# Third layer of a four-layer graph network: signals once per column pair or chunk, and the sum's own wait placed ahead of the fill

## The chip, the cores and the metric

One core of one Trainium2 chip. The metric is the device time of one execution in microseconds (us), as a median of runs. A core has five engines with queues of their own: TensorE (PE, matmuls), VectorE (DVE), ScalarE (ACT), GpSimd (POOL, which here issues the indirect transfers) and SyncE (SP, which issues the plain ones). They meet only through semaphores: an instruction may add one to a semaphore when it ends (`then_inc`), and a queue may stand until a semaphore has reached a number (`wait_ge`).

## The reference

Four graph layers run one after the other over 6250 nodes and 106250 edges that are sorted by destination; each adds its input and normalises. The change lies in the third, an attention with six heads:

```python
gl = (x @ W_l).reshape(n, H, F_OUT)
gr = (x @ W_r).reshape(n, H, F_OUT)
s = jax.nn.leaky_relu(gl[src] + gr[dst], NEG_SLOPE)
e = jnp.einsum('ehf,hf->eh', s, att)
m = jax.ops.segment_max(e, dst, num_segments=n)
p = jnp.exp(e - m[dst])
denom = jax.ops.segment_sum(p, dst, num_segments=n)
alpha = p / (denom[dst] + 1e-16)
msg = alpha[:, :, None] * gl[src]
out = jax.ops.segment_sum(msg, dst, num_segments=n)
```

## The kernel before

The edges lie as 128 rows (partitions) of 832 columns, and each layer walks over them in 52 chunks of 16 columns. In the third layer a chunk c passes through these stations.

GpSimd (`layer2_g`, `g2_chunk`) gathers the 64 source features of each column with one indirect transfer per column into one of five buffers XS. It waits until the buffer's last use is over, by semaphores p2 (DVE) and ap (ACT). SyncE loads the destination features that stand at the first edge of each node (`x2_chunk`).

DVE fills the destination features of the other edges (`fill2`, L1191): column j is column j - 1 times a flag plus the loaded value, so each depends on the one before. Fills run four chunks ahead of the sums. Their semaphore is f2.

TensorE transposes four columns at a time (`pt_t`, L1205), multiplies them with the weights (`pm_t`, L1220, three times), and sums up the heads' logits (`pe_t`, L1236, then `pf_t`, L1251). ACT drains each of these banks (L1212, L1227, L1244, L1256); the last hands over the logits by semaphore ab.

DVE makes the softmax of a chunk in six steps (`soft2`, L1306 to L1320, semaphore q2), a running maximum forth and back over the columns among them. ACT takes two exponentials of it (`exp2_a`, L1329 and L1330, semaphore ax) and copies the maxima into the result (L1335, semaphore am).

The features are then scaled with each head's weight into a result S2 of 16 x 396 numbers a row, twice buffered: four heads by DVE in products of two columns (`px2`, L1354, semaphore p2), two heads by ACT, one copy per column and head (`px2_a`, L1371, semaphore ap). DVE makes running sums over the columns (`step2`, L1385; for a chunk's first column L1383 after the carry L1342), each dependent on the one before, semaphore t2. SyncE stores the 3168 KB of the chunk.

The order is written out by hand. DVE's (`layer2_v`) per column of chunk c is: fill of chunk c + 4, sum of chunk c, on even columns the product of the next pair, and in columns 8 to 13 one softmax step of chunk c + 1. From chunk 48 on there are no fills. ACT's (`layer2_a`) is eighteen places per chunk with the bank drains of chunk c + 3, and between them 33 instructions of `px2_a`, so that column j's two copies lie at about place 18 (2j + 3) / 33; ab is given at place 10. In the order before a fill waits for the fill before it, and a sum for its products, its own column's copies and the sum before it, in this order behind the fill:

```python
for j in range(CH):
    if c + 4 < NCH:
        fill2(e, c + 4, j)
    step2(e, c, j)
    if j % 2 == 0 and j + 2 < CH:
        px2(e, c, j // 2 + 1)
```

Of the kernel before, what the change touches and what calls it, by code (L numbers as in the profile page):

```python
# [7 lines left out]
D = 64  # L8
# [65 lines left out]
def bc(a, shape):  # L74
    return a.broadcast_to(shape)
# [6 lines left out]
def build(nc, x, src, dst, et16, et8, w0, beta, wl, wr, att, bias2, w3, coeff, hbias, loopw, out):  # L82
# [22 lines left out]
    with ExitStack() as ctx:  # L105
        names = ["tu", "m3", "e8", "ata", "att", "ao", "ab", "ae", "am", "ap", "ar", "at", "ax", "bad", "bb", "edges", "f1", "f2", "fin", "fina", "flag", "fr",
# [1051 lines left out]
        def q2_at(c):  # L1158
            return 6 * c - 2 if c else 0

        def p2_end(c):

            return 9 * c + 8

        def g2_chunk(e, c):
            if c >= NX:
                e.wait_ge(S["p2"], p2_end(c - NX))
                e.wait_ge(S["ap"], 33 * (c - NX + 1))
            for j in range(CH):
                gather(xsv(c)[:, j, 0:D], xt2, Si[:, c * CH + j:c * CH + j + 1], f"g_{2 * (c % NX) + j // 8}")  # L1170

        def x2_chunk(e, c):
            if c >= 3:
                e.wait_ge(S["f2"], 16 * (c - 3) + 15)
            load(e, XB2[:, c % 3, :], xdv[:, c * CH:(c + 1) * CH, :].rearrange("p j d -> p (j d)"), f"x_{c % 3}")

        def fill2(e, c, j):
            if c == 0 and j == 0:
                return
            cur, prv = xsv(c), xsv(c - 1)  # L1180
            XBv = XB2[:, c % 3, :].rearrange("p (j d) -> p j d", j=CH)
            if c == 0 and j == 1:
                e.wait_ge(S["xdi"], 32)
            if j == 0 or (c == 0 and j == 1):
                e.wait_ge(S[f"x_{c % 3}"], 16 * len(range(c % 3, NCH, 3)) + 16 * (c // 3 + 1))
                if c >= NX:
                    e.wait_ge(S["p2"], p2_end(c - NX))
                    e.wait_ge(S["ap"], 33 * (c - NX + 1))
            if c or j > 1:
                e.wait_ge(S["f2"], 16 * c + j - 1)  # L1190
            v.scalar_tensor_tensor(out=cur[:, j, D:P], in0=cur[:, j - 1, D:P] if j else prv[:, CH - 1, D:P],  # L1191
                                   scalar=gf[:, c * CH + j:c * CH + j + 1], in1=XBv[:, j, :],
                                   op0=ALU.mult, op1=ALU.add).then_inc(S["f2"], 1)

        def pt_t(e, u):
# [4 lines left out]
            if q == 0:  # L1200
                e.wait_ge(S["f2"], 16 * c + 15)
# [44 lines left out]
        def pf_t(e, c):  # L1246
            e.wait_ge(S["ae"], c + 1)
            if c:
                e.wait_ge(S["q2"], q2_at(c - 1) + (5 if c > 1 else 4))
            for i in range(4):  # L1250
                m = t.transpose(PS[7][:, i * P:(i + 1) * P], ETs[:, i * P:(i + 1) * P], ident[:])  # L1251
            m.then_inc(S["pf"], 1)
# [39 lines left out]
        def soft2(e, c, i):  # L1292
# [5 lines left out]
            n = q2_at(c) + (i - 1 if c == 0 and i else i)  # L1298
            if n:
                e.wait_ge(S["q2"], n)  # L1300
            if i == 0:
                e.wait_ge(S["ab"], c + 1)
                e.wait_ge(S["bb"], 1)
                if c:
                    e.wait_ge(S["am"], c)
# [16 lines left out]
            m.then_inc(S["q2"], 1)  # L1322

        def exp2_a(e, c):
            n_ = H * (CH + 1) if c else H * CH
            e.wait_ge(S["q2"], q2_at(c + 1))
            if c:
                e.wait_ge(S["p2"], p2_end(c - 1))
            s.activation(pw2[:, 0:n_], pf2[:, c % 2, 0:n_], ACT.Exp).then_inc(S["ax"], 1)  # L1329
# [5 lines left out]
            s.copy(s2v(c)[:, :, HW:].rearrange("p j h -> p h j"), mb2).then_inc(S["am"], 1)  # L1335

        def carry2(e, c):

            pq = pw2[:, H * CH:H * CH + H]
            e.wait_ge(S["ax"], 2 * c + 1)  # L1340
# [4 lines left out]
        def px2(e, c, k):  # L1345
# [4 lines left out]
            if k == 0:  # L1350
                e.wait_ge(S["ax"], 2 * c + 1)
                if c >= 2:
                    e.wait_ge(S[f"s_{c % 2}"], stored_before(2, c % 2) + 16 * (c // 2))
            v.tensor_tensor(s2v(c)[:, cols, 0:n * 65].rearrange("p j (h d) -> p j h d", h=n)[:, :, :, 0:D],  # L1354
                            bc(xsv(c)[:, cols, 0:D].unsqueeze(2), [P, 2, n, D]),
                            bc(pe_[:, cols, 0:n].unsqueeze(3), [P, 2, n, D]), ALU.mult).then_inc(S["p2"], 1)

        def px2_a(e, c, i):

            Sv, pe_ = s2v(c), p2v(c)  # L1360
            if i == 0:
                if c >= 2:
                    e.wait_ge(S[f"s_{c % 2}"], stored_before(2, c % 2) + 16 * (c // 2))
                    e.wait_ge(S["p2"], p2_end(c - 2) + 1)
                e.wait_ge(S["ax"], 2 * c + 2)
                s.copy(Sv[:, :, 0:HW].rearrange("p j (h d) -> p j h d", h=H)[:, :, :, D].rearrange("p j h -> p h j"),
                       pe_).then_inc(S["ap"], 1)
# [3 lines left out]
            s.activation(Sv[:, j, h * 65:h * 65 + D], xsv(c)[:, j, 0:D], ACT.Copy, scale=pe_[:, h, j:j + 1]).then_inc(S["ap"], 1)  # L1371

        def step2(e, c, j):
            if c == 0 and j == 0:
                return
            Sv = s2v(c)
            if j % 2 == 0 or (c == 0 and j == 1):
                e.wait_ge(S["p2"], p2_end(c) - 7 + j // 2)
            e.wait_ge(S["ap"], 33 * c + 1 + 2 * (j + 1))
            if c or j > 1:  # L1380
                e.wait_ge(S["t2"], 16 * c + j - 1)
# [8 lines left out]
        def layer2_v(e):  # L1390
# [7 lines left out]
            for c in range(NCH):  # L1398
# [3 lines left out]
                for j in range(CH):  # L1402
                    if c + 4 < NCH:
                        fill2(e, c + 4, j)
                    step2(e, c, j)
                    if j % 2 == 0 and j + 2 < CH:
                        px2(e, c, j // 2 + 1)
                    if c + 1 < NCH and j >= CH - 8 and j - (CH - 8) < 6:
                        soft2(e, c + 1, j - (CH - 8))
                    if c == NCH - 1 and j < 13:  # L1410
                        if j == 0:
                            e.wait_ge(S["am"], NCH)
# [43 lines left out]
        def layer2_y(e):  # L1456
# [4 lines left out]
            for c in range(NCH):  # L1461
                if c + 5 < NCH:
                    x2_chunk(e, c + 5)
                e.wait_ge(S["am"], c + 1)
# [858 lines left out]
```

## Time and profile before

| | |
|---|---|
| runs | 4820.8, 4825.5, 4825.6 us, median 4825.5 us |
| profiled execution, span from first to last instruction | 6172.5 us (a time around the span is not given) |
| busy in it | PE 1601.1, DVE 2873.7, ACT 1131.4, POOL 3511.2 us |
| third layer in it | about 3100 to 4750 us |
| DMA | 529.62 MB, mean 86 GB/s |

The profiled execution is 28% longer than the runs, so its durations of single instructions and its waits have to be told apart: the table's first line is what is to be forecast, and the rows below are from the second. A line of the timeline is a start, a length and an operation, with the idle time of the engine ahead of it in brackets. A length runs from start to the confirmed end; the next instruction of an engine may start before that. So the pace of an engine is read from start to start.

### The profile page before, as it was taken

Reading aid. Unit: us, or ns where it says so; the run is one execution under the profiler, and the core shown is the slowest. Engines: PE = TensorE matmul, PEld = TensorE weight load, DVE = VectorE, ACT = ScalarE, POOL = GpSimd, SP = SyncE. Lnnn points to the kernel's source line nnn. Section 1 sums busy time; section 2 is a strip of 40 time slices with the busy share of each in tenths; the row PEclk is TensorE's granted clock in tenths of the full one; section 3 lists DMA queues with packets and bytes.
Section 4 is the critical chain, followed back from the end, with each engine's and each line's share of the span. In section 5 each row is a group of like instructions: output and inputs, shape, how many; then the busy total and the mean of one; then the engine's idle time right before and its main releaser. Section 6 shows DMA issues by size and latency. Waiting matters only on the chain.

```text
span 6172.5 us, 31606 instructions
## 1 busy us (share of the span) xinstructions
PE 1601.1 (26%) x6543; PEld 810.8 (13%) x6543; DVE 2873.7 (47%) x7569; ACT 1131.4 (18%) x3424; POOL 3511.2 (57%) x3636
## 2 busy tenths in 40 slices
PE   5531110000000000003376566656564500000002
PEld 1421110000000000001122222222221400000001
DVE  2344444124345455444255555555556632443435
ACT  1100000000000000001155555555555500000000
POOL 4356666756666666664634544454452576666764
PEclk7765555555555555556688888888887655555555
DMA  4211222221222222221123333333334221222222
GB/s 139 106 53 62 67 64 71 67 81 54 58 64 71 62 69 68 64 71 37 49 106 118 140 138 123 130 139 134 118 140 154 69 67 55 64 79 63 79 63 78
DMA packets 185944, 529.62 MB, mean 86 GB/s; under 512 B 70454, under 2 KB 75170, under 8 KB 169480
## 3 DMA queue, kind: packets, MB, share of 16 engines
q1 hardware_dynamic: 65816, 395.51, 16.9%
q0 software_dynamic: 117696, 129.81, 9.2%
q10 hardware_dynamic: 2224, 2.13, 0.1%
q14 instruction: 151, 1.24, 0.1%
q8 instruction: 57, 0.93, 0.1%
HBM read 185.57 MB, written 341.44 MB: 85 GB/s over the span
## 4 chain that ended last, share of the span: by engine, by line
DVE 39%; another core or an unknown queue 27%; issue 14%; PE 11%; ACT 6%; POOL 3%; DMA 0%; DVEq 0%; ACTq 0%; POOLq 0%
DVE AR L1672 11%; DVE AR L514 5%; DVE ps L779 5%; PE ps L1220 4%; POOL AR L190 2%; ACT AR L1371 2%; PE ps L1236 2%; DVE AR L850 2%; DVE AR L1385 2%; ACT AR L1227 1%; DVE AR L364 1%; DVE AR L1662 1%; PE ps L680 1%; DVE AR L803 1%
## 5 line engine op out<-in xcount | busy, mean ns | idle before, releaser
L190 POOL DMA_INDIRECT AR<-xt,Si x2496 | 2404.4, 963 | 1715.2 <-issue 744.3
L190 POOL DMA_INDIRECT AR<-y,R x752 | 711.3, 946 | 531.1 <-issue 228.7
L1385 DVE SCALAR_TENSOR_TENSOR AR<-AR,gf 128x390 f32<-128x390 f32 x780 | 484.2, 621 | 665.8 <-ACT AR L1371 469.9
L1220 PE MATMUL ps<-AR,WLR 128*128 128x512 f32 x1248 | 690.3, 680 | 152.2 <-ACT AR L1227 113.0
L1672 DVE SCALAR_TENSOR_TENSOR AR<-AR,gf 128x128 f32<-128x128 f32 x831 | 295.0, 355 | 470.8 <-DVE AR L1672 386.9
L1371 ACT ACTIVATE AR<-AR 128x64 f32<-128x64 f32 x1664 | 495.4, 346 | 0.0
L1227 ACT ACTIVATE AR<-ps 128x512 f32<-128x512 f32 x624 | 368.5, 591 | 231.3 <-remote 168.1
L779 DVE SCALAR_TENSOR_TENSOR ps<-ps,gf,AR 128x64 f32<-128x64 f32 x831 | 241.9, 291 | 288.2 <-remote 168.4
L514 DVE SCALAR_TENSOR_TENSOR AR<-AR,gf 128x64 f32<-128x64 f32 x831 | 237.2, 285 | 263.6 <-DVE AR L514 173.3
L190 POOL DMA_INDIRECT AR<-s,endi x196 | 215.7, 1101 | 179.5 <-issue 113.4
L1220 PEld LDWEIGHTS ps<-AR,WLR 128*128 128x128 f32 x1248 | 242.2, 218 | 462.2 <-issue 342.1
L1354 DVE TENSOR_TENSOR AR<-AR,ps 128x512 f32<-128x512 f32 x416 | 282.8, 680 | 6.7 <-ACT ps L1329 6.7
L850 DVE SCALAR_TENSOR_TENSOR AR<-AR,gf 128x65 f32<-128x65 f32 x780 | 217.2, 278 | 95.9 <-remote 58.0
L1191 DVE SCALAR_TENSOR_TENSOR AR<-AR,gf 128x64 f32<-128x64 f32 x831 | 229.7, 276 | 48.5 <-DVE AR L1191 20.4
L828 ACT ACTIVATE ps<-AR 128x17 f32<-128x17 f32 (+1 forms) x52 | 9.8, 188 | 1262.0 <-remote 602.9
L364 DVE TENSOR_TENSOR AR<-AR,ps 128x1568 bf16<-128x1568 int32 x52 | 92.7, 1784 | 302.9 <-remote 279.9
L372 PE MATMUL ps<-AR 128*98 128x64 bf16 x832 | 80.1, 270 | 547.3 <-DVE AR L366 419.8
L1742 PE MATMUL ps<-ident,AR 128*128 128x128 f32 x1 | 0.5, 475 | 808.7 <-DVE AR L1672 808.7
L1991 ACT ACTIVATE AR<-AR 128x7 f32<-128x7 f32 x7 | 1.5, 208 | 1113.0 <-DVE AR L632 1050.4
L1236 PE MATMUL ps<-AR,A 128*32 128x512 f32 x1248 | 204.9, 604 | 0.0
L1016 PE MATMUL ps<-AR,ones 128*128 128x384 f32 (+1 forms) x6 | 3.7, 759 | 718.6 <-DVE AR L967 718.6
L883 PE MATMUL ps<-AR,ones 128*128 128x128 f32 x2 | 0.8, 502 | 698.3 <-DVE AR L868 698.3
(326 smaller groups left out, 3045.4 us busy)
## 6 DMA issues: line engine op xcount, KB each, us to landing
s<-AR SPq DMA_DIRECT2D x51, 3168.0 KB
AR<-xd SPq DMA_DIRECT2D x104, 512.0 KB
s<-AR SPq DMA_DIRECT2D x51, 1024.0 KB
AR<-xt,Si POOLq DMA_INDIRECT x2496
s<-AR SPq DMA_DIRECT2D x53, 512.0 KB
s<-AR SPq DMA_DIRECT2D x51, 528.0 KB
xd<-AR SPq DMA_DIRECT2D x52, 512.0 KB
y<-AR SPq DMA_DIRECT2D x24, 1024.0 KB
```

What stands on the lines that cost most here:

```text
L190: g.indirect_dma_start(out=o, out_offset=None, in_=table, in_offset=bass.IndirectOffsetOnAxis(ap=idx, axis=0)).then_inc(S[sem], 16)
L514: v.scalar_tensor_tensor(out=buf[:, j, :], in0=buf[:, j - 1, :] if j else prev[:, CH - 1, :], scalar=gf[:, c * CH + j:c * CH + j + 1], in1 ...
L779: v.scalar_tensor_tensor(out=xf1(c, j), in0=xf1(c, j - 1) if j else xf1(c - 1, CH - 1), scalar=gf[:, c * CH + j:c * CH + j + 1], in1=XBv[: ...
L850: v.scalar_tensor_tensor(out=Sv[:, j, 0:65], in0=Sv[:, j - 1, 0:65] if j else Sp[:, CH - 1, 0:65], scalar=gf[:, c * CH + j:c * CH + j + 1] ...
L1191: v.scalar_tensor_tensor(out=cur[:, j, D:P], in0=cur[:, j - 1, D:P] if j else prv[:, CH - 1, D:P], scalar=gf[:, c * CH + j:c * CH + j + 1] ...
L1220: t.matmul(PS[2 + k % 3][:], WLR[:, ch * P:(ch + 1) * P], XT2[:, u % 6, :], start=True, stop=True).then_inc(S["pm"], 1)
L1227: s.activation(RL2[:, u % 5, ch * 512:(ch + 1) * 512], PS[2 + k % 3][:], ACT.Relu).then_inc(S["ar"], 1)
L1236: m = t.matmul(PS[6][32 * q:32 * q + 32, :], w_, m_, start=(ch == 0), stop=(ch == 3))
L1354: v.tensor_tensor(s2v(c)[:, cols, 0:n * 65].rearrange("p j (h d) -> p j h d", h=n)[:, :, :, 0:D], bc(xsv(c)[:, cols, 0:D].unsqueeze(2), [P ...
L1371: s.activation(Sv[:, j, h * 65:h * 65 + D], xsv(c)[:, j, 0:D], ACT.Copy, scale=pe_[:, h, j:j + 1]).then_inc(S["ap"], 1)
L1385: m = v.scalar_tensor_tensor(out=Sv[:, j, 0:HW], in0=Sv[:, j - 1, 0:HW], scalar=gf[:, c * CH + j:c * CH + j + 1], in1=Sv[:, j, 0:HW], op0= ...
L1672: v.scalar_tensor_tensor(out=cur[:, j, :], in0=cur[:, j - 1, :] if j else prv[:, CH - 1, :], scalar=gf[:, c * CH + j:c * CH + j + 1], in1= ...
```

## The change

Inside the third layer signals are dropped and those left stand for more. A product signals only for the first and last pair of a chunk (three p2 steps a chunk with the carry, nine before). Of the scaled copies only the last of a pair of columns signals (8 a chunk, 33 before), and the sum of an even column waits for both columns' copies. Fills from the sixth chunk on signal once a chunk. Of the softmax only the last step signals, of the two exponentials the second, and semaphore am is gone. What is dropped is covered by the wait for the sum before: that wait now stands at the head of each column, ahead of the fill and the softmax step, and the softmax step has moved from behind the sum and product to ahead of the sum.

```diff
-        def q2_at(c):
-            return 6 * c - 2 if c else 0
+        def f2_at(c):
+
+            return 16 * c + 15 if c < 5 else 75 + c
 
         def p2_end(c):
 
-            return 9 * c + 8
+            return 3 * c + 2
 
         def g2_chunk(e, c):
             if c >= NX:
                 e.wait_ge(S["p2"], p2_end(c - NX))
-                e.wait_ge(S["ap"], 33 * (c - NX + 1))
+                e.wait_ge(S["ap"], 8 * (c - NX + 1))
...
             if c >= 3:
-                e.wait_ge(S["f2"], 16 * (c - 3) + 15)
+                e.wait_ge(S["f2"], f2_at(c - 3))
...
                     e.wait_ge(S["p2"], p2_end(c - NX))
-                    e.wait_ge(S["ap"], 33 * (c - NX + 1))
-            if c or j > 1:
+                    e.wait_ge(S["ap"], 8 * (c - NX + 1))
+            if c < 5 and (c or j > 1):
                 e.wait_ge(S["f2"], 16 * c + j - 1)
-            v.scalar_tensor_tensor(out=cur[:, j, D:P], in0=cur[:, j - 1, D:P] if j else prv[:, CH - 1, D:P],
-                                   scalar=gf[:, c * CH + j:c * CH + j + 1], in1=XBv[:, j, :],
-                                   op0=ALU.mult, op1=ALU.add).then_inc(S["f2"], 1)
+            m = v.scalar_tensor_tensor(out=cur[:, j, D:P], in0=cur[:, j - 1, D:P] if j else prv[:, CH - 1, D:P],
+                                       scalar=gf[:, c * CH + j:c * CH + j + 1], in1=XBv[:, j, :],
+                                       op0=ALU.mult, op1=ALU.add)
+            if c < 5 or j == CH - 1:
+                m.then_inc(S["f2"], 1)
...
-                e.wait_ge(S["f2"], 16 * c + 15)
+                e.wait_ge(S["f2"], f2_at(c))
...
-                e.wait_ge(S["q2"], q2_at(c - 1) + (5 if c > 1 else 4))
+                e.wait_ge(S["q2"], c)
...
-            n = q2_at(c) + (i - 1 if c == 0 and i else i)
-            if n:
-                e.wait_ge(S["q2"], n)
+            if c == 0:
+                vc.hold()
             if i == 0:
                 e.wait_ge(S["ab"], c + 1)
                 e.wait_ge(S["bb"], 1)
-                if c:
-                    e.wait_ge(S["am"], c)
                 m = v.tensor_copy(Bf[:, :, 1:CH], bc(Bn[:, c * CH + 1:(c + 1) * CH].unsqueeze(1), [P, H, CH - 1]))
...
                 m = v.scalar_tensor_tensor(out=pq, in0=Sp[:, CH - 1, HW:], scalar=Bn[:, c * CH:c * CH + 1],
                                            in1=mb2[:, :, 0], op0=ALU.add, op1=ALU.subtract)
-            m.then_inc(S["q2"], 1)
+            if i == (5 if c else 4):
+                m.then_inc(S["q2"], 1)
+            elif c == 0:
+                vc.up(m)
...
             n_ = H * (CH + 1) if c else H * CH
-            e.wait_ge(S["q2"], q2_at(c + 1))
+            e.wait_ge(S["q2"], c + 1)
             if c:
                 e.wait_ge(S["p2"], p2_end(c - 1))
-            s.activation(pw2[:, 0:n_], pf2[:, c % 2, 0:n_], ACT.Exp).then_inc(S["ax"], 1)
+            s.activation(pw2[:, 0:n_], pf2[:, c % 2, 0:n_], ACT.Exp)
             s.activation(pf2[:, c % 2, 0:n_], pf2[:, c % 2, 0:n_], ACT.Exp).then_inc(S["ax"], 1)
             if c >= 2:
                 e.wait_ge(S[f"s_{c % 2}"], stored_before(2, c % 2) + 16 * (c // 2))
             if c >= 2:
                 e.wait_ge(S["p2"], p2_end(c - 2) + 1)
-            s.copy(s2v(c)[:, :, HW:].rearrange("p j h -> p h j"), mb2).then_inc(S["am"], 1)
+            s.copy(s2v(c)[:, :, HW:].rearrange("p j h -> p h j"), mb2)
...
-            e.wait_ge(S["ax"], 2 * c + 1)
+            e.wait_ge(S["ax"], c + 1)
...
             if k == 0:
-                e.wait_ge(S["ax"], 2 * c + 1)
+                e.wait_ge(S["ax"], c + 1)
...
+            m = v.tensor_tensor(s2v(c)[:, cols, 0:n * 65].rearrange("p j (h d) -> p j h d", h=n)[:, :, :, 0:D],
+                                bc(xsv(c)[:, cols, 0:D].unsqueeze(2), [P, 2, n, D]),
+                                bc(pe_[:, cols, 0:n].unsqueeze(3), [P, 2, n, D]), ALU.mult)
+            if k in (0, CH // 2 - 1):
+                m.then_inc(S["p2"], 1)
...
+                e.wait_ge(S["ax"], c + 1)
+                s.copy(Sv[:, :, 0:HW].rearrange("p j (h d) -> p j h d", h=H)[:, :, :, D].rearrange("p j h -> p h j"), pe_)
...
+            m = s.activation(Sv[:, j, h * 65:h * 65 + D], xsv(c)[:, j, 0:D], ACT.Copy, scale=pe_[:, h, j:j + 1])
+            if j % 2 and h == H - 1:
+                m.then_inc(S["ap"], 1)
 
         def step2(e, c, j):
             if c == 0 and j == 0:
                 return
             Sv = s2v(c)
+            if j == 0 or (c == 0 and j == 1):
+                e.wait_ge(S["p2"], p2_end(c) - 1)
             if j % 2 == 0 or (c == 0 and j == 1):
-                e.wait_ge(S["p2"], p2_end(c) - 7 + j // 2)
-            e.wait_ge(S["ap"], 33 * c + 1 + 2 * (j + 1))
-            if c or j > 1:
-                e.wait_ge(S["t2"], 16 * c + j - 1)
+                e.wait_ge(S["ap"], 8 * c + j // 2 + 1)
...
                 for j in range(CH):
+                    if c or j > 1:
+                        e.wait_ge(S["t2"], 16 * c + j - 1)
                     if c + 4 < NCH:
                         fill2(e, c + 4, j)
+                    if c + 1 < NCH and j >= CH - 8 and j - (CH - 8) < 6:
+                        soft2(e, c + 1, j - (CH - 8))
                     step2(e, c, j)
                     if j % 2 == 0 and j + 2 < CH:
                         px2(e, c, j // 2 + 1)
-                    if c + 1 < NCH and j >= CH - 8 and j - (CH - 8) < 6:
-                        soft2(e, c + 1, j - (CH - 8))
                     if c == NCH - 1 and j < 13:
-                        if j == 0:
-                            e.wait_ge(S["am"], NCH)
                         mend_max_v(e, vc, 2, T2, H, B2, j)
...
             for c in range(NCH):
                 if c + 5 < NCH:
                     x2_chunk(e, c + 5)
-                e.wait_ge(S["am"], c + 1)
                 n = CH // 4 if c == NCH - 1 else CH
                 for j in range(0, CH, n):
                     e.wait_ge(S["t2"], 16 * c + j + n - 1)
```

## Rows read from the trace of the kernel before

**Rows 1.** the page: totals of the engines, and the busy tenths in 40 slices

```profile
PE 1601.1 (26%) x6543; PEld 810.8 (13%) x6543; DVE 2873.7 (47%) x7569; ACT 1131.4 (18%) x3424; POOL 3511.2 (57%) x3636
DVE  2344444124345455444255555555556632443435
POOL 4356666756666666664634544454452576666764
```

**Rows 2.** GpSimd's waits over the whole span: waiting instruction, releaser, total us, times, longest

```profile
POOL AR L190 <- issue: 1111.0, 3414, 55.9
POOL AR L190 <- ACT AR L1371: 607.3, 47, 52.3
POOL AR L190 <- DMA s<-AR: 171.3, 7, 92.7
POOL AR L190 <- DMA y<-AR: 84.2, 1, 84.2
POOL AR L190 <- DMA xt<-X: 49.0, 1, 49.0
```

**Rows 3.** timeline of GpSimd in the third layer: start, length, operation

```profile
3601.71 0.94 POOL L190 DMA_INDIRECT AR<-xt,Si  x1 [0.30 <-issue]
3602.96 0.94 POOL L190 DMA_INDIRECT AR<-xt,Si  x1 [0.31 <-issue]
```

**Rows 4.** waits of all engines, 3150 to 4650 us

```profile
DVE AR L1385 <- ACT AR L1371: 450.7, 122, 10.6
ACT AR L1244 <- remote: 365.8, 46, 11.0
```

**Rows 5.** timeline of DVE in a dense stretch of the third layer

```profile
3615.07 0.35 DVE L1311 TENSOR_TENSOR_SCAN AR<-AR 128x96 f32<-128x96 f32 x1
...
3618.52 0.22 DVE L1320 SCALAR_TENSOR_TENSOR AR<-AR,Bn 128x6 f32<-128x6 f32 x1
3618.66 0.27 DVE L1191 SCALAR_TENSOR_TENSOR AR<-AR,gf 128x64 f32<-128x64 f32 x1
3618.86 0.61 DVE L1385 SCALAR_TENSOR_TENSOR AR<-AR,gf 128x390 f32<-128x390 f32 x1
3619.39 0.28 DVE L1191 SCALAR_TENSOR_TENSOR AR<-AR,gf 128x64 f32<-128x64 f32 x1
3619.59 0.61 DVE L1385 SCALAR_TENSOR_TENSOR AR<-AR,gf 128x390 f32<-128x390 f32 x1
3620.31 0.57 DVE L1342 TENSOR_TENSOR ps<-AR,ps 128x390 f32<-128x390 f32 x1
3620.79 0.68 DVE L1354 TENSOR_TENSOR AR<-AR,ps 128x512 f32<-128x512 f32 x1
3621.38 0.28 DVE L1191 SCALAR_TENSOR_TENSOR AR<-AR,gf 128x64 f32<-128x64 f32 x1
3621.58 0.55 DVE L1383 TENSOR_TENSOR AR<-AR,ps 128x390 f32<-128x390 f32 x1
3622.05 0.68 DVE L1354 TENSOR_TENSOR AR<-AR,ps 128x512 f32<-128x512 f32 x1
```

**Rows 6.** timeline of DVE in the fourth layer

```profile
5411.81 6.17 DVE L1672 SCALAR_TENSOR_TENSOR AR<-AR,gf 128x128 f32<-128x128 f32 x16
...
5504.00 0.35 DVE L1672 SCALAR_TENSOR_TENSOR AR<-AR,gf 128x128 f32<-128x128 f32 x1 [1.00 <-DVE AR L1672]
```

**Rows 7.** timeline of ACT beside rows 5

```profile
3618.26 0.37 ACT L1371 ACTIVATE AR<-AR 128x64 f32<-128x64 f32 x1
3618.77 0.26 ACT L1329 ACTIVATE ps<-AR 128x102 f32<-128x102 f32 x1
3618.97 0.27 ACT L1330 ACTIVATE AR<-AR 128x102 f32<-128x102 f32 x1
...
3621.20 0.57 ACT L1227 ACTIVATE AR<-ps 128x512 f32<-128x512 f32 x1
...
3622.15 0.58 ACT L1227 ACTIVATE AR<-ps 128x512 f32<-128x512 f32 x1
```

More of the change, by code:

```diff
@@ L105, in build @@
     with ExitStack() as ctx:
-        names = ["tu", "m3", "e8", "ata", "att", "ao", "ab", "ae", "am", "ap", "ar", "at", "ax", "bad", "bb", "edges", "f1", "f2", "fin", "fina", "flag", "fr",
+        names = ["tu", "m3", "e8", "ata", "att", "ao", "ab", "ae", "ap", "ar", "at", "ax", "bad", "bb", "edges", "f1", "f2", "fin", "fina", "flag", "fr",
                  "i0", "init", "kn", "lp", "ma", "mp", "mv", "n0", "n1", "n3", "na", "oe", "of", "ofo", "or", "orl", "ot",
@@ L1350, in px2 @@
             if k == 0:
-                e.wait_ge(S["ax"], 2 * c + 1)
+                e.wait_ge(S["ax"], c + 1)
                 if c >= 2:
                     e.wait_ge(S[f"s_{c % 2}"], stored_before(2, c % 2) + 16 * (c // 2))
-            v.tensor_tensor(s2v(c)[:, cols, 0:n * 65].rearrange("p j (h d) -> p j h d", h=n)[:, :, :, 0:D],
-                            bc(xsv(c)[:, cols, 0:D].unsqueeze(2), [P, 2, n, D]),
-                            bc(pe_[:, cols, 0:n].unsqueeze(3), [P, 2, n, D]), ALU.mult).then_inc(S["p2"], 1)
+            m = v.tensor_tensor(s2v(c)[:, cols, 0:n * 65].rearrange("p j (h d) -> p j h d", h=n)[:, :, :, 0:D],
[3 more added lines that the diff above has]
+                m.then_inc(S["p2"], 1)
         def px2_a(e, c, i):
@@ L1364, in px2_a @@
                     e.wait_ge(S["p2"], p2_end(c - 2) + 1)
-                e.wait_ge(S["ax"], 2 * c + 2)
-                s.copy(Sv[:, :, 0:HW].rearrange("p j (h d) -> p j h d", h=H)[:, :, :, D].rearrange("p j h -> p h j"),
-                       pe_).then_inc(S["ap"], 1)
+                e.wait_ge(S["ax"], c + 1)
+                s.copy(Sv[:, :, 0:HW].rearrange("p j (h d) -> p j h d", h=H)[:, :, :, D].rearrange("p j h -> p h j"), pe_)
                 return
@@ L1370, in px2_a @@
             h += HV
-            s.activation(Sv[:, j, h * 65:h * 65 + D], xsv(c)[:, j, 0:D], ACT.Copy, scale=pe_[:, h, j:j + 1]).then_inc(S["ap"], 1)
+            m = s.activation(Sv[:, j, h * 65:h * 65 + D], xsv(c)[:, j, 0:D], ACT.Copy, scale=pe_[:, h, j:j + 1])
+            if j % 2 and h == H - 1:
+                m.then_inc(S["ap"], 1)
         def step2(e, c, j):
```

## The prediction

> **What bounds the kernel now.** I read the totals and the forty slices first [rows 1]. GpSimd, which issues the gathers, is busy longest, 57% of the span. VectorE (DVE) follows with 47%. In the slices of the third layer (about 3100 to 4750 us, the stretch where DVE shows 5 and POOL 4 to 5) neither is near full. So the third layer, as profiled, waits for something else than its own busy time.
>
> The waits of that stretch say for what [rows 4]. DVE stands 450.7 us for ScalarE's (ACT) scaled copies at L1371, and ACT stands 365.8 us, 46 times in 46 chunks, before the copy at L1244 for a releaser that the trace does not name. That copy waits for TensorE alone. A chunk so takes 1500 / 46 = 32.6 us.
>
> I don't take it that this stands in an execution without the profiler. The span is 6172.5 us, the median of the runs 4825.5 us, so 1347 us exist only under the profiler. Another row shows such a stretch by itself: in the fourth layer sixteen sums, each waiting for the one before, take 6.17 us, and a little later the same instruction begins 1.00 us after its forerunner ended [rows 6]. DVE itself slows there for no reason in the code. I take TensorE's late signals for the same thing and look for the bound in the dense stretches, between the stalls.
>
> There the pace per chunk of 16 columns is this.
> GpSimd: one gather every 1.25 us (3601.71 to 3602.96) [rows 3], so 16 x 1.25 = 20.0 us.
> DVE: from start to start, a fill to the sum behind it takes 0.20 us, a sum to the next fill 0.53, a product to what follows 0.59, the carry 0.48, the softmax steps 0.14 to 0.27 (six of them, 1.1 together), and the last sum to the carry 0.72 [rows 5]. With 16 fills, 14 sums at 0.53, one at 0.72, the first column's at 0.47, 8 products and the carry: 3.2 + 7.4 + 0.7 + 0.5 + 4.7 + 0.5 + 1.1 = 18.1 us.
> ACT: one drain of a bank and two scaled copies in 0.95 us (3621.20 to 3622.15) [rows 7], 16 times, 15.2 us, and by estimate 1.3 us for the six single instructions of a chunk (0.2 us each as from L1329 to L1330 [rows 7], more for L1244): 16.5 us.
>
> How much of GpSimd's 20 us is real? GpSimd has 3636 instructions, all but a few of them transfers [rows 1]. Waits that no layer's pace can hide are 171.3, 84.2 and 49.0 us for transfers, and the longest single ones of L1371 and of "issue", 52.3 and 55.9 us: 412.7 us together [rows 2]. If the gathers set the pace elsewhere, one takes (4825.5 - 412.7) / 3636 = 1.21 us, and a chunk 19.4 us. That lies 1.3 us above DVE's 18.1. So my reading is: GpSimd sets the pace of the third layer, with DVE close behind.
>
> **The change part by part.**
> *Signals dropped* (most products, most scaled copies, fills from the sixth chunk on, five of six softmax steps, am, one of two ax). In the dense rows each instruction begins 0.03 to 0.1 us before the end of the one ahead, signal or not waited for [rows 5]. A signal is sent at an instruction's end, beside the next one. I find nothing to win, and take 0.
>
> *Waits dropped on DVE* (f2, q2, and for most columns p2 and ap). In the dense rows they are met long before: fills follow at 0.53 us behind a 0.61 us sum, the softmax step at 3618.52 right behind its sum [rows 5]. Saving 0. Bounds: no loss, as a wait less can't delay; a gain of at most the reading error of these rows, 0.01 us an instruction, which over 46 instructions and 47 chunks is 22 us, and only if DVE set the pace.
>
> *The sum's own wait moved ahead of the fill.* This is the part with a price. Today column j's fill stands between sum j-1 and the wait for it, and overlaps the sum's end. Now the fill queues behind the wait. Behind an even column a product lies in between (0.59 us), which hides it. Behind an odd column nothing does: 7 places per chunk (columns 2, 4 to 14; before column 0 lie the carry and a product). What such a wait costs has two rows. The chain of the fourth layer has (6.17 - 0.35) / 15 = 0.39 us from start to start for 0.35 us of work [rows 6], so length plus 0.04; a sum of 0.61 to 0.62 would be followed at 0.65 instead of 0.53: 0.12 us. The last sum before the carry is followed at 0.72 [rows 5]: 0.19 us, but that one waits for two semaphores. I take 0.12, since the fill waits for one. 7 x 0.12 = 0.84 us per chunk, 18.1 becomes 18.9. There are 47 chunks with fills behind chunk 0, so 39 us on DVE, 62 us by the upper row, and none if the fill could not overlap the sum in the first place. The four last chunks have no fills; there the wait stood in this place already.
>
> The rows show an instruction that starts 0.08 us before the sum ahead of it ends [rows 5]. The Trainium skill, VectorE: DVE Perf Modes, section "The DRAIN you can't avoid", says that the next operation does not start until the pipe is empty, and that dropping semaphores gains nothing. By the first half the moved wait would cost 0 and not 0.84 us per chunk. The trace speaks against that half. With the second half it agrees.
>
> *Softmax steps ahead of the sum, not behind.* Their number and length stay. The last one now ends one sum (0.53 us) earlier. In exchange it no longer shields the fill behind odd columns, which is counted above.
>
> Its first step also waits for the logits (ab) and now has column 8's sum and product queued behind it, which were ahead of it. ACT hands over ab at place 10 of its order and column 8's copies only after it, so the sum would stand there anyway: 0.
>
> *Pairs of scaled copies.* An even column now waits for both columns' copies, two more copies and perhaps a drain, up to 0.95 us [rows 7]. Both sums then run at once. While DVE is behind ACT nothing is lost. At a chunk's start the second pair of copies ends at about 3622.2, and the first column's sum begins at 3621.58 [rows 5, 7]; the softmax's end 0.53 us earlier makes up for it. Left is a delay of up to 1 us, once, ahead of the last pair of sums.
>
> *ax once*: the carry now waits for the second exponential, ended at about 3619.3, and starts at 3620.31 anyway. 0. *SP's wait for am dropped*: the store waits for the chunk's last sum, later anyhow. 0. *x2 loads and TensorE's f2 waits* name the same last fill. 0. *TensorE's wait for q2* ahead of L1251 names the step one column later; ACT's drain L1244, which it waits for too, stands in ACT's queue behind the exponential of that very softmax. 0. *p2 and ap for releasing a gather buffer* name the same last product and copy. 0.
>
> **Sum.** GpSimd's 19.4 us per chunk stay, DVE goes from 18.1 to 18.9 below it, the tail gets about 1 us. In the profiled execution it is no more: DVE stands 450.7 us idle for ACT in the stretch [rows 4], and 0.84 x 46 = 39 us go into that. Span 6172.5 plus 1; time 4825.5 plus 1.5, **4827 us**. A difference under 0.2% (9.7 us) is about what measurements of this kernel can't tell from none.
>
> **Rivals.**
> *A, slower: DVE sets the pace of the third layer.* Place: seven fills per chunk behind the moved wait. For it: DVE is within 1.3 us of GpSimd, by a division that assumes that gathers pace all other layers; where other layers have idle time too, a gather takes less than 1.21 us, and at 18.1 / 16 = 1.13 us DVE is even. From 18.9 / 16 = 1.18 us on it begins to cost. Against it: the profiled rate is 1.25. Price 47 x 0.84 = 39 us: 4865 us; between 1.13 and 1.18 a part of it.
> *B, faster: ACT's wait for the softmax lies on the path.* Its copy starts at 3618.26, the next could start 0.24 us later, and the exponential starts at 3618.77, right behind the last softmax step: 0.27 us of idleness [rows 7]. The step comes 0.53 us earlier now, so that goes. Should ACT's order of work set the pace (through TensorE's banks), 51 x 0.27 = 14 us are won: 4812 us. Against it: ACT's 16.5 us are the least of the three.
> *C: the trace's stall is real.* If TensorE's late signals stand outside the profiler too, all three engines have some 12 us per chunk to spare, and the time stays at 4825 us. It is a part of "same".
>
> **How the numbers follow.** My forecast with C 0.50, A 0.32, B 0.18. The range goes from B's 4810 to A's 4866. Faster by over 0.2%: 0.18; within: 0.50; slower: 0.32.
>
> **What would show it.** In the profile after, DVE's dense stretch should have a fill 0.65 us behind an odd column's sum instead of 0.53, 0.20 from fill to sum unchanged, and 0.6 behind a product. The gathers keep their 1.25 us. The exponential L1329 should no longer stand behind the softmax's last step. If the time falls by more than 14 us, signals or met waits have a price that these rows do not show. If it rises by more than 39, the wait for pairs has one. If fills follow odd sums at 0.53 still, my term is void.

## The result, and the profile after

Before: 4823.16 us (median of 4 runs, 4819.81 to 4825.64). After: 4790.42 us (4 runs, 4789.92 to 4791.97). The ratio is 0.9939, 95% interval 0.9927 to 0.9950: 33 us faster, where 4827 and a range from 4810 up were forecast. The changed kernel taken once more (e7) gave 4784.51 against 4814.37 us, ratio 0.9939 [0.9922, 0.9955].

One thing first, without which the numbers can't be read: within a set of runs taken together on one chip, the kernel before takes either 4808 to 4826 us or some 6030 to 6190 us, in each run of the set, and the profiled execution before the prediction looks like one of the second kind. I say quick and slow chips for short, though it isn't shown to be a property of the chip: e16 (slow) and e17 (quick), 12 minutes apart, both ran on what is numbered chip 9, which may or may not be the same one. A new profile of the kernel before, on a quick chip (e8), is what the changed kernel is set against here. (The two come from different sets, in which before took 4813.6 and 4823.2 us.) Totals of the engines, GpSimd's busy tenths in 40 slices and the gathers' group, kernel before on a quick chip:

```profile
span 4811.9 us, 31606 instructions
PE 1460.2 (30%) x6543; PEld 739.3 (15%) x6543; DVE 2848.1 (59%) x7569; ACT 1131.6 (24%) x3424; POOL 3536.0 (73%) x3636
POOL 6777777777777777776777777777744777777776
L190 POOL DMA_INDIRECT AR<-xt,Si x2496 | 2416.8, 968 | 809.3 <-issue 757.9
```

The same of the changed kernel:

```profile
span 4788.2 us, 30757 instructions
PE 1454.7 (30%) x6543; PEld 751.3 (16%) x6543; DVE 2862.1 (60%) x7569; ACT 1123.5 (23%) x3424; POOL 3508.8 (73%) x3636
POOL 6777777777777777776777777777654777777776
L190 POOL DMA_INDIRECT AR<-xt,Si x2496 | 2386.1, 956 | 811.5 <-issue 755.2
```

849 instructions are gone (31606 to 30757), yet DVE is not less busy. What fell is GpSimd's busy time, by 27 us, with the same 3636 instructions. From the first running sum of the third layer to the last go 1084.8 us before (2448.7 to 3533.5) and 1053.8 after (2451.9 to 3505.7): 31 us less. The gain lies there. The wait of [rows 2] for L1371, 607.3 us, is gone on a quick chip: from 2500 to 3400 us, inside the third layer, GpSimd stands for other engines 2 us before and 6 us after. Its groups of instructions in that stretch (count | busy us, mean ns | idle time before), first before (e8), then after:

```profile
L190 POOL DMA_INDIRECT AR<-xt,Si x686 | 692.7, 1010 | 209.1 <-issue 206.9 <-ACT AR L1371 2.1
```

```profile
L190 POOL DMA_INDIRECT AR<-xt,Si x710 | 683.9, 963 | 216.8 <-issue 210.9 <-DVE ps L1345 5.7 <-ACT AR L1375 0.3
```

Between two gathers lie the same 0.30 us in both. In 900 us after has 24 gathers more, for one reason: a gather takes 963 ns on average and not 1010. With 48 chunks of 16 gathers, 768 x 0.047 = 36 us. Summed gather by gather from 2450 to 3480 us, what they take beyond 945 ns is 50.4 us before and 15.8 after. GpSimd does set the pace, as forecast, but its pace depends on something that the change moves.

Answering to [rows 3] and [rows 5], the timeline of GpSimd and DVE in the kernel before on a quick chip (start, length; the wait of an engine in brackets):

```profile
2924.31 0.63 DVE L1385 SCALAR_TENSOR_TENSOR AR<-AR,gf 128x390 f32<-128x390 f32 x1 [0.78 <-ACT AR L1371]
2925.20 0.94 POOL L190 DMA_INDIRECT AR<-xt,Si  x1 [0.30 <-issue]
...
2927.50 0.62 DVE L1385 SCALAR_TENSOR_TENSOR AR<-AR,gf 128x390 f32<-128x390 f32 x1 [2.23 <-issue]
2927.70 1.25 POOL L190 DMA_INDIRECT AR<-xt,Si  x1 [0.30 <-issue]
...
2929.09 0.62 DVE L1385 SCALAR_TENSOR_TENSOR AR<-AR,gf 128x390 f32<-128x390 f32 x1
2929.25 1.47 POOL L190 DMA_INDIRECT AR<-xt,Si  x1 [0.30 <-issue]
...
2929.62 0.35 DVE L1314 TENSOR_TENSOR_SCAN AR<-AR 128x96 f32<-128x96 f32 x1
...
2938.54 0.62 DVE L1385 SCALAR_TENSOR_TENSOR AR<-AR,gf 128x390 f32<-128x390 f32 x1
2938.95 1.02 POOL L190 DMA_INDIRECT AR<-xt,Si  x1 [0.30 <-issue]
```

A gather with no sum under its start takes 0.94 us. One that starts 0.20 us after a sum takes 1.25 (0.31 more), one 0.41 us after 1.02. The one 0.16 us after a sum takes 1.47, but there a softmax step with two inputs in SBUF, the running maximum back over the columns (L1314), follows directly on the sum. And the changed kernel:

```profile
2906.12 0.68 DVE L1357 TENSOR_TENSOR AR<-AR,ps 128x512 f32<-128x512 f32 x1
2906.50 0.95 POOL L190 DMA_INDIRECT AR<-xt,Si  x1 [0.31 <-issue]
2906.91 0.62 DVE L1390 SCALAR_TENSOR_TENSOR AR<-AR,gf 128x390 f32<-128x390 f32 x1
2907.57 0.28 DVE L1192 SCALAR_TENSOR_TENSOR AR<-AR,gf 128x64 f32<-128x64 f32 x1
2907.75 0.95 POOL L190 DMA_INDIRECT AR<-xt,Si  x1 [0.30 <-issue]
2907.77 0.62 DVE L1390 SCALAR_TENSOR_TENSOR AR<-AR,gf 128x390 f32<-128x390 f32 x1
...
2919.84 0.22 DVE L1320 SCALAR_TENSOR_TENSOR AR<-AR,Bn 128x6 f32<-128x6 f32 x1
2919.98 0.62 DVE L1390 SCALAR_TENSOR_TENSOR AR<-AR,gf 128x390 f32<-128x390 f32 x1
2920.10 0.26 ACT L1332 ACTIVATE ps<-AR 128x102 f32<-128x102 f32 x1 [0.91 <-DVE AR L1320]
```

A sum that starts 0.02 us after the gather costs it nothing, nor does a product (one input in SBUF, one in PSUM) that starts 0.38 us ahead of one. The fill follows its sum at 0.66 us, as forecast. Sorted by where the sum starts against the gather over 2500 to 3400 us, the mean length of a gather in the kernel before is 1028 ns for a sum 0.45 to 0.40 us ahead, 1101 for 0.35 to 0.30, 1231 for 0.25 to 0.20, 1422 for 0.20 to 0.15, and 944 to 945 for sums 0.10 us ahead to 0.05 us behind.

One rule fits nearly all of them: the gather ends 0.94 us after a point that lies 0.48 to 0.50 us behind the sum's start (161 of the 187 gathers with a sum 0.10 to 0.45 us ahead). So the less the lead, the longer the gather. Where L1314 follows on the sum, that point lies 0.69 to 0.70 us behind its start (22 of 23 cases); 16 of the 21 gathers in the place with 1422 ns are such. The changed kernel has none of these, for its softmax step stands ahead of the sum.

In the changed kernel (e7, another profile of it) the cheap half of the costly places is as full as before (85 sums 0.45 to 0.40 or 0.35 to 0.30 us ahead, 93 before), but the dear half is nearly empty: 4 sums 0.25 to 0.10 us ahead, where before had 80.

That was a correlation in two traces. The Trainium skill, "SBUF — State Buffer", section "Who interferes with whom", says that a DVE instruction with two SBUF inputs contends with a GpSimd instruction that reads SBUF, and that issue order decides who blocks. The sum has two such inputs. A gather reads its indices (Si) there. These traces show one side only: a sum holds up a gather, but sums that start while a gather runs last 0.62 us like all others, and a sum less than 0.10 us ahead of a gather doesn't hold it.

### The profile page after: what moved, and what is told of

It reads as the page before. It is cut to its first block and busy times, and to the rows that moved or that the text cites. A ratio compares the mean times of both kernels' runs of the same rounds, so it can differ in the third digit from the quotient of the medians.

```text
span 4788.2 us, 30757 instructions
## 1 busy us (share of the span) xinstructions
PE 1454.7 (30%) x6543; PEld 751.3 (16%) x6543; DVE 2862.1 (60%) x7569; ACT 1123.5 (23%) x3424; POOL 3508.8 (73%) x3636
## 5 line engine op out<-in xcount | busy, mean ns | idle before, releaser
L190 POOL DMA_INDIRECT AR<-y,R x752 | 723.6, 962 | 238.1 <-issue 218.1
L1223 PE MATMUL ps<-AR,WLR 128*128 128x512 f32 x1248 | 609.4, 612 | 72.8 <-ACT AR L1230 72.8
L1666 DVE TENSOR_TENSOR AR<-AR,ps 128x2048 f32<-128x2048 f32 (+1 forms) x53 | 119.1, 2248 | 545.0 <-DMA AR<-xt,Si 545.0
L800 DVE TENSOR_TENSOR AR<-AR,ps 128x512 f32<-128x512 f32 x104 | 66.9, 684 | 437.2 <-DMA AR<-xt,Si 437.2
L1357 DVE TENSOR_TENSOR AR<-AR,ps 128x512 f32<-128x512 f32 x416 | 283.0, 680 | 6.8 <-ACT AR L1333 6.8
L190 POOL DMA_INDIRECT AR<-s,endi x196 | 215.9, 1101 | 76.7 <-issue 65.8
L1223 PEld LDWEIGHTS ps<-AR,WLR 128*128 128x128 f32 x1248 | 214.4, 192 | 324.1 <-issue 237.5
```

The source lines that it names most:

```text
L190: g.indirect_dma_start(out=o, out_offset=None, in_=table, in_offset=bass.IndirectOffsetOnAxis(ap=idx, axis=0)).then_inc(S[sem], 16)
L1223: t.matmul(PS[2 + k % 3][:], WLR[:, ch * P:(ch + 1) * P], XT2[:, u % 6, :], start=True, stop=True).then_inc(S["pm"], 1)
L1357: m = v.tensor_tensor(s2v(c)[:, cols, 0:n * 65].rearrange("p j (h d) -> p j h d", h=n)[:, :, :, 0:D], bc(xsv(c)[:, cols, 0:D].unsqueeze(2) ...
```

## The experiments

Two theories in the end, in the expectations from e12 on. S: sums with two SBUF inputs that start just ahead of a gather hold it up; the change moved them. G: signals and waits cost time themselves. The expectations of e1 to e11 were written before this was seen and use other letters: W says that ACT's wait for the softmax is a link of the loop that sets the pace, and S there is what is called G later.

**First round, slow chip** (before 6054.66 us, 15 runs; e1 itself 6062.85).

> The kernel before, unchanged, for a second profile that is hopefully not stretched. Theory W (ACT's wait for the softmax ahead of the exponential is a link of the loop DVE - ACT - TensorE): a chunk of the third layer takes 20.9 us (20.24 us of after plus 33 us / 48), GpSimd has to wait for the release of a buffer in most chunks, and ACT stands longer before L1329 than the 0.9 us of after, some 1.5 us. Theory S (the signals themselves cost time on ACT or DVE): ACT's copies or DVE's sums stand further apart from start to start than in after (0.24 and 0.53 us there).

The softmax step alone moved ahead of the sum and product:

```diff
                     if c + 4 < NCH:
                         fill2(e, c + 4, j)
+                    if c + 1 < NCH and j >= CH - 8 and j - (CH - 8) < 6:
+                        soft2(e, c + 1, j - (CH - 8))
                     step2(e, c, j)
...
-                    if c + 1 < NCH and j >= CH - 8 and j - (CH - 8) < 6:
-                        soft2(e, c + 1, j - (CH - 8))
```

> The kernel before with one thing of the change alone: the softmax step stands ahead of the sum and product of its column instead of behind them, all signals and waits kept. Theory W: nearly the whole gain, -25 to -35 us (4790 to 4798). Theory S: nothing, within 5 us of before.

Only the scaled copies signal once per pair of columns:

```diff
-            s.activation(Sv[:, j, h * 65:h * 65 + D], ...).then_inc(S["ap"], 1)
+            m = s.activation(Sv[:, j, h * 65:h * 65 + D], ...)
+            if j % 2 and h == H - 1:
+                m.then_inc(S["ap"], 1)
...
-            e.wait_ge(S["ap"], 33 * c + 1 + 2 * (j + 1))
+            if j % 2 == 0 or (c == 0 and j == 1):
+                e.wait_ge(S["ap"], 8 * c + j // 2 + 1)
```

> The kernel before with ACT's scaled copies signalling once per pair of columns (8 a chunk instead of 33) and the sum of an even column waiting for the pair, nothing else. Theory W: no gain, 0 to +10 us, as an even column starts later. Theory S: -10 to -33 us.

Only the wait for the sum before moved ahead of the fill:

```diff
                 for j in range(CH):
+                    if c or j > 1:
+                        e.wait_ge(S["t2"], 16 * c + j - 1)
                     if c + 4 < NCH:
                         fill2(e, c + 4, j)
...
-            if c or j > 1:
-                e.wait_ge(S["t2"], 16 * c + j - 1)
```

> The kernel before with the wait for the sum before moved ahead of the fill, nothing else. By the price of my prediction (0.12 us in 7 places of 47 chunks): +39 us if DVE is in the loop that sets the pace, which theory W says, so +20 to +45 us. Theory S with DVE off the path: 0.

Measured: softmax ahead 1.0084 [1.0056, 1.0112], pairs 0.9983 [0.9973, 0.9994], wait ahead 1.0075 [1.0050, 1.0100]. A single part made the kernel slower here, though the whole makes it faster on a quick chip. Why a slow chip's times don't answer the question shows in e1's waits, 3100 to 4200 us:

```profile
POOL AR L190 <- ACT AR L1371: 357.4, 35, 11.3
DVE AR L1385 <- ACT AR L1371: 276.8, 105, 8.9
ACT AR L1244 <- remote: 219.7, 33, 10.0
```

DVE stands for ACT's copies, ACT for something unnamed ahead of the copy of TensorE's logits (L1244), and GpSimd for 357 us of 1100; the gathers don't set the pace. Another slow chip (before 6177.64 us, 11 runs):

> The kernel before, unchanged, a look. On a chip that runs it in about 4823 us, theory W: 20.9 us per chunk of the third layer (after: 20.24), GpSimd waiting for buffers in most chunks, ACT standing about 1.5 us ahead of L1329 (after: 0.9). Theory S: ACT's copies or DVE's sums further apart than 0.24 and 0.53 us. On a chip that takes about 6050 us again: stalls as in the profile before, and no answer.

> The softmax step ahead of the sum, all signals and waits kept, once more. On a chip with before at about 4823 us, theory W: -25 to -35 us. Theory S: within 5 us. On a chip with before at about 6050 us: +0.8% again, as in e2.

e5 took 6188.08 us, e6 1.0041 [1.0026, 1.0057].

**Quick chips.** The changed kernel again:

> The changed kernel itself. On a chip with before at 4823 us: 4790 us again. On a chip with before at 6050 to 6180 us, where e2 to e6 were run: soft_early and wait_ahead gave +0.4 to +0.8% there and pairs -0.2%. If the change is the sum of its parts, after is 0 to +1.4% there; theory W, in which GpSimd's 20.2 us limit what can be gained on a quick chip and the stalls of the late signals rule on a slow one, says slower or the same; theory S (fewer signals are less work wherever signals are slow) says clearly faster there, by 1% or more.

4784.51 us, 0.9939 [0.9922, 0.9955]. It repeats the gain, with a span of 4779.8 us. Then, in one set of runs (before 4813.60 us, 22 runs), the kernel before in profile, the softmax step ahead, the pairs, and the changed kernel with its softmax step put back behind the sum (for which it keeps its own six q2 signals):

> The kernel before, unchanged, a look, hoped for on a chip that runs it in about 4820 us. Theory W: 20.9 us per chunk of the third layer (after: 20.24), GpSimd waiting for buffers in most chunks, ACT standing about 1.5 us ahead of L1329 (after: 0.9). Theory S: ACT's copies or DVE's sums further apart than 0.24 and 0.53 us.

> Before with the softmax step ahead of the sum, nothing else. With before at about 4820 us, theory W: -25 to -35 us. Theory S: within 5 us.

> Before with ACT's copies signalling once per pair, nothing else. With before at about 4820 us, theory W: 0 to +10 us. Theory S: -10 to -33 us.

```diff
...
+                    step2(e, c, j)
+                    if j % 2 == 0 and j + 2 < CH:
+                        px2(e, c, j // 2 + 1)
                     if c + 1 < NCH and j >= CH - 8 and j - (CH - 8) < 6:
                         soft2(e, c + 1, j - (CH - 8))
-                    step2(e, c, j)
-                    if j % 2 == 0 and j + 2 < CH:
-                        px2(e, c, j // 2 + 1)
```

> After with the softmax step put back behind the sum and product, where it stood before, and its own signals and waits with it; all else as in after. With before at about 4820 us, theory W: the gain is gone, 4815 to 4860 us (the wait ahead of the fill costs without its counterpart). Theory S: 4785 to 4792 us, the gain stays.

e8 took 4813.78 us, e9 4808.48, e10 4821.88, e11 4801.19. Each kernel's mean gather, 2500 to 3400 us, gives its span to some 7 us (e7 and e17 are from other sets of runs, in which before took 4814.37 and 4815.41 us). The estimate is 768 gathers times the difference to e8's 1010 ns:

| kernel | mean gather, ns | estimate, us | span to e8's 4811.9, us | third layer, us | ratio of times |
|---|---|---|---|---|---|
| e10 pairs | 1011 | +1 | +2.6 | 1091.8 | 1.0018 [1.0008, 1.0028] |
| e8 before | 1010 | 0 | 0 | 1084.8 | 1 |
| e9 softmax ahead | 994 | -12 | -9.7 | 1074.7 | 0.9992 [0.9982, 1.0002] |
| e11 after, softmax behind | 982 | -22 | -14.6 | 1071.4 | 0.9976 [0.9965, 0.9987] |
| e17 (below) | 968 | -32 | -26.4 | 1056.5 | 0.9947 [0.9930, 0.9963] |
| e7 changed kernel | 962 | -37 | -32.1 | 1052.5 | 0.9939 [0.9922, 0.9955] |

The pairs alone drop 25 of 33 signals a chunk and win nothing; the runs are 8 us longer, the span 3. The softmax step's place alone took 10 us off the span in the profiled execution, but only 5 off the median, which isn't clear of noise (0.9982 to 1.0002). With the rest of the change around it, it is worth 17 us (e11 to e7).

Theory W falls: it expected 25 to 35 us from e9 and no gain left in e11, and in e8 GpSimd stands 2 us of 900 for buffers, not in most chunks. The S of these expectations falls with e10, of which it expected 10 to 33 us. e11, at 4801.19 us, lies between what the two expected.

**Taking the cause away.** Everything of the kernel before stays, signals and waits too, but in columns 1 to 12 one input of the sum comes from PSUM. (The sum then leaves the scaled copies out in those columns.)

```diff
-                                           ..., in1=Sv[:, j, 0:HW],
+                in1 = bc(pw2[:, 0:1], [P, HW]) if j <= CH - 4 else Sv[:, j, 0:HW]
+                                           ..., in1=in1,
```

> The kernel before with one input of the sum in the third layer changed: in columns 1 to 12 of a chunk it adds one column of the exponentials, which lie in PSUM, in place of the scaled copies, so that only one of its inputs lies in SBUF (this leaves the sum over the scaled copies out of those columns; they are still written and still waited for). Same operation, same 390 elements, same waits and signals. Theory S (a sum that starts 0.1 to 0.5 us ahead of a gather holds it up until the sum has read its two SBUF inputs): gathers are held up in 4 of 16 columns at most, their mean length falls from 1.010 to about 0.96 us, and the kernel takes about 4780 us, 30 to 35 less than before, with every signal of before in its place. Theory G (the signals and waits themselves cost the time, and the gathers are long for a reason of their own): the mean stays at 1.00 to 1.01 us and the time within 0.2% of before.

> The same edit of the sum on the changed kernel (columns 1 to 12 leave the scaled copies out). Theory S: its gathers had only 0.30 us a chunk of delay left, so little is to be had: mean length 0.963 to about 0.95 us, time 4775 to 4785 us, and less than 10 us between this kernel and the same edit on the kernel before, where the two without the edit differ by 29. Theory G: the two still differ by about 29 us.

> The kernel before with one thing moved: the sum's wait for the sum before it stands ahead of the fill, every signal kept, as the change has it. Theory S: the fill starts 0.12 us later after each sum, which shifts the sums against the gathers but does nothing else; gathers' mean length between 0.98 and 1.01 us, time 4800 to 4820. If the wait's place alone made the changed kernel faster: 4790.

> The kernel before with both of the change's moves (the wait ahead of the fill, the softmax step ahead of the sum) and with every signal of before kept. Theory S has it that signals matter only through the places at which the sums start: with the order of the changed kernel but the waits of before, the mean length of a gather comes out between 0.963 and 0.994 us and the time between 4790 and 4808, and the two follow one line with the other kernels (some 42 us for each us of delay in a chunk). If signals cost time of their own: over 4808 at a delay of the gathers like the changed kernel's.

This was a slow chip once more (before 6058.28 us, 18 runs). Ratios: e12 1.0232 [1.0183, 1.0282], e13 1.0109 [1.0073, 1.0145], e14 1.0073 [1.0051, 1.0095], e15 1.0024 [1.0007, 1.0040]; all the times expected were for quick chips and are void. The lengths of the gathers still answer. Their means, 3100 to 4200 us, are 991 ns in e1 and 990 in e3 (pairs), but 974 in e4 and e14 (wait ahead), 972 in e2 (softmax ahead) and 982 in e15 (both): with every signal kept, either move alone changes how far the gathers are held up. GpSimd's group, 3100 to 4200 us, e1 and then e12:

```profile
L190 POOL DMA_INDIRECT AR<-xt,Si x574 | 568.6, 991 | 525.8 <-ACT AR L1371 357.4 <-issue 168.4
```

```profile
L190 POOL DMA_INDIRECT AR<-xt,Si x522 | 495.5, 949 | 646.8 <-ACT AR L1371 493.7 <-issue 153.1
```

991 falls to 949 ns. All that gathers take beyond 945 ns fell from 26.9 to 3.1 us. A sum 0.25 to 0.15 us ahead stretched a gather to 1205 and 1274 ns in e1, and to 944 in e12. So the hold-up comes from the second SBUF input. What it is worth needed a quick chip:

> The kernel of e12 again (the kernel before with one SBUF input of the sum in columns 1 to 12 replaced by a column in PSUM, which leaves the scaled copies out of the sum there), to have its time where the gathers set the pace. On the other chip the edit took the delay of the gathers from 26.9 to 3.1 us in 1100 us of the third layer. Theory S: mean length of a gather 0.945 to 0.96 us against 1.010, third layer 1040 to 1055 us against 1085, time about 4780 us against 4814, with every signal of before. Theory G: within 0.2% of before.

Slow again (before 6055.83; 1.0226 [1.0195, 1.0258]).

> The kernel of e12 and e16 once more (the kernel before with one SBUF input of the sum in columns 1 to 12 replaced by a column in PSUM, which leaves the scaled copies out of the sum there), for a chip on which the gathers set the pace. Theory S there: mean length of a gather 0.945 to 0.96 us against 1.010, third layer 1040 to 1055 us against 1085, time about 4780 us against 4814. Theory G: within 0.2% of before. On a chip like that of e16 (before about 6055 us), both expect what e16 gave, 1.02 times before, with gathers of 0.949 us.

A quick chip: 4788.35 us against 4815.41 (7 runs), ratio 0.9947 [0.9930, 0.9963], 27 us faster. Theory G, which expected the time within 0.2% of before, falls. Groups of GpSimd and of the sum, and the timeline of e17:

```profile
L190 POOL DMA_INDIRECT AR<-xt,Si x708 | 685.3, 968 | 215.8 <-issue 210.9 <-ACT AR L1371 4.3 <-DVE AR L1354 0.6
L1386 DVE SCALAR_TENSOR_TENSOR AR<-AR,gf,ps 128x390 f32<-128x390 f32 x531 | 328.8, 619 | 78.5 <-ACT AR L1371 54.0 <-issue 24.2
```

```profile
2907.75 0.62 DVE L1386 SCALAR_TENSOR_TENSOR AR<-AR,gf,ps 128x390 f32<-128x390 f32 x1 [0.41 <-ACT AR L1371]
2907.88 0.94 POOL L190 DMA_INDIRECT AR<-xt,Si  x1 [0.30 <-issue]
...
2917.54 0.61 DVE L1386 SCALAR_TENSOR_TENSOR AR<-AR,gf 128x390 f32<-128x390 f32 x1
2917.87 1.09 POOL L190 DMA_INDIRECT AR<-xt,Si  x1 [0.30 <-issue]
```

The sum is as long as before (619 ns, before 622), and yet one that starts 0.13 us ahead of a gather leaves it at 0.94 us. In column 15, where both inputs still lie in SBUF, a lead of 0.33 us gives 1.09. The same holds for the whole 900 us of this one trace: of the gathers that start 0.10 to 0.45 us after a sum, the 157 behind a sum with an input in PSUM take 0.94 to 0.96 us, and the 43 behind a sum with both in SBUF 1.03 to 1.39, 1.20 on average. That shows the cause. The time falls a little short of the 4780 us expected: the mean stayed at 968 ns, not under 960. Two thirds of what is left comes from these 43 in columns 13 to 15.

> The kernel of e13 again (the changed kernel with one SBUF input of the sum in columns 1 to 12 replaced by a column in PSUM, which leaves the scaled copies out of the sum there). On the quick kind of chip, where the kernel before takes about 4815 us, the same edit made that kernel 27 us faster, though every signal of it stood. Theory S: the changed kernel had little delay of gathers left, so it gains under 10 us by the edit (4780 to 4790 us), and the two edited kernels lie within 8 us of each other, where the unedited ones lie 29 to 33 us apart. Theory G: the two edited kernels are still 29 us apart (about 4760 us). On the other kind of chip (before about 6055 us) both expect what e13 gave, 1.011 times before.

This too met a slow chip (before 6059.32; 1.0077 [1.0051, 1.0103], mean gather 955 ns). So whether the two kernels come out equal once the cause is taken from both wasn't seen on a quick chip.

## Why the prediction was wrong, point by point

**GpSimd sets the pace: right.** It has 0.30 us between gathers and no wait to speak of in both kernels.

**A chunk of 19.4 us in the kernel before: the step that failed.** I divided the time by the number of transfers and got one rate, 1.21 us, for the whole kernel and for both versions. Undisturbed, a gather comes each 1.25 us, as [rows 3] said. In the third layer of the kernel before it came each (692.7 + 209.1) / 686 = 1.31 us, which is 21.0 us a chunk, and after each (683.9 + 216.8) / 710 = 1.27 us, 20.3 a chunk. So the term "GpSimd's 19.4 us per chunk stay" was wrong twice: it was 21.0 and not 19.4, and it didn't stay but fell by 0.7 us. Over 48 chunks that is 34 us, and that is the miss; my sum had no term by which the change could reach GpSimd's pace. The trace of before had it: the gathers' group from 3150 to 4650 us has a mean of 988 ns where [rows 3] show 0.94, and its timeline shows one of the long ones just behind the stretch of [rows 5]. The group first, then the timeline, both of the kernel before as profiled for the prediction:

```profile
L190 POOL DMA_INDIRECT AR<-xt,Si x738 | 729.0, 988 | 771.6 <-ACT AR L1371 555.0 <-issue 216.5
```

```profile
3625.68 0.63 DVE L1385 SCALAR_TENSOR_TENSOR AR<-AR,gf 128x390 f32<-128x390 f32 x1
...
3625.83 1.29 POOL L190 DMA_INDIRECT AR<-xt,Si  x1 [0.31 <-issue]
```

I took the clean rows for the pace and didn't ask what made the others longer.

**"1347 us exist only under the profiler": wrong.** On quick chips the profiled executions span 4779.8 to 4814.5 us, and on a slow one the kernel before takes 6033 to 6072 us in all 18 runs of a set. The stalls of [rows 4] and [rows 6] are a slow chip's: in the fourth layer's chain of [rows 6] 417 of 778 sums come 1.4 us after the one ahead, in e1 420, and in e8 none (0.5 at most). To read the pace from the dense stretches was sound; the reason given for it was not.

**The moved wait costs 0.12 us behind an odd column: right in size, and half the story.** From sum to fill the median start-to-start went from 0.535 to 0.654 us. It is the one term that I had as a loss, and rival A made 39 us of it. DVE did not set the pace: it still waits 45.8 us in 900 for the scaled copies (before 65.0). And a delay of DVE is not only a cost here, since it moves the sums against the gathers. I had also taken the Trainium skill, VectorE: DVE Perf Modes, section "The DRAIN you can't avoid", to be contradicted by the rows. The same section goes on to say that a next operation that isn't held starts earlier, and the 0.535 us behind a sum of 0.62 us agree with that.

**Dropped signals and waits are worth 0: upheld, not proven.** ACT's copies follow each other at 0.24 us with and without them, and e10 gained nothing from 25 signals less; the other dropped signals were never tried by themselves. e17, with all signals, has its third layer within 3 to 4 us of the changed kernel's (1056.5 to 1052.5 and 1053.8), and these fit the 6 ns between the mean gathers.

**Rival B, faster by ACT's wait: wrong mechanism.** It had the sign by luck: it said that the wait before the exponential goes, and it grew: in 900 us from 1.6 us to

```profile
ACT ps L1332 <- DVE AR L1320: 39.6, 44, 1.0
```

44 times 0.9 us, and the kernel is faster all the same. **Rival C** named stalls that quick chips don't have.

**What stays open.** Why this order makes the sums land in harmless places. Nearly all of the changed kernel's chunks repeat at 20.2 or 20.3 us, those of before wander between 19.5 and 23.7. That the softmax step's place enters is seen in e9 and e11; the moved wait by itself was seen to change the gathers on slow chips only (e4, e14), and so was the order of the changed kernel with all signals kept (e15). I had no way to foretell the places. Nor is it known what makes a chip slow, or why there most kernels with shorter gathers took longer.

## What to carry to other kernels

When the engine that sets the pace shows unequal lengths for equal instructions, sort them by what another engine does at their start before taking any of them for its rate. An edit that costs the other engine time can still win, if it moves that engine's instructions with two SBUF inputs away from the stretch just ahead of the pacing ones. And look at the clean and the mean length side by side: here 0.94 against 0.99 us was the whole case.

## What the runs showed of the hardware

- A sum of 390 elements with two inputs in SBUF that starts 0.10 to 0.45 us ahead of a gather on GpSimd holds it up until 0.48 to 0.50 us behind the sum's start in 161 of 187 cases of e8, so by 0.05 to some 0.4 us, and a sum less than 0.10 us ahead does not. With one input in PSUM the same sum does nothing to it (e12, e17). The rule of the Trainium skill on two SBUF inputs, cited above, agrees, and here issuing an indirect gather behaves as a GpSimd instruction that reads SBUF.
- Instructions with two SBUF inputs in close succession add up. With L1314 directly behind the sum the hold ends 0.69 to 0.70 us behind the sum's start. The two longest gathers of e8, 1.59 us, start between a fill 0.11 us ahead of them and a sum 0.09 us behind. In the changed kernel 43 gathers lie in such a place and take 0.97 to 1.03 us; why these get through between the two isn't known.
- On slow chips DVE's instructions have the same lengths (the sum 622 ns in e8, 620 in e1), but TensorE's are longer (L1220 621 ns at a granted clock of 0.98 of full in the third layer of e8, 690 at 0.85 in that of e1), and an engine may stand over 1 us for the end of its own last instruction. Whether the clock is a cause or a consequence isn't known. The fourth layer's chain, e1:

```profile
5270.65 0.35 DVE L1672 SCALAR_TENSOR_TENSOR AR<-AR,gf 128x128 f32<-128x128 f32 x1 [1.06 <-DVE AR L1672]
5272.04 0.35 DVE L1672 SCALAR_TENSOR_TENSOR AR<-AR,gf 128x128 f32<-128x128 f32 x1 [1.04 <-DVE AR L1672]
```

  1.39 us from start to start, where [rows 6] also have 0.39, and e8 never more than 0.5.
